# Two reorderings behind a two-layer expert stage: a transpose of gates moved behind one layer 1, a fold and a layer 2 moved ahead of the last layer 1

## The reference, cut to what matters

```python
x = x + attention(channel_layernorm(x))
t = tokens(x);  xt = layernorm(t)                  # the input of router and experts
probs = softmax(xt @ Wr + br); top_p, top_idx = top_k(probs, 2); weights = top_p / top_p.sum()
xn = layernorm(xt);  xe = xn * ln_g[e] + ln_b[e]   # for each expert e
h = gelu(xe @ W1[e] + b1[e]);  y[e] = h @ W2[e] + b2[e]
t = t + (weights[..., None] * y_tok[top_idx]).sum()
```

## Time and profile before

| what | us |
|---|---|
| median of 3 runs | 58.93 (58.92 to 59.0) |
| the profiled execution | 59.4 |
| its span from first to last instruction | 57.6 |
| PE busy | 50.3 (87%) |
| DVE busy | 40.9 (71%) |
| ACT busy | 35.4 (62%) |
| POOL busy | 24.8 (43%) |

### The profile page before, as it was taken

The page is one execution under the profiler, slowest core; times in us unless marked ns, Lnnn a source line. Parts: engine busy times, 40 slices in busy tenths (PEclk is TensorE's granted clock), DMA queues, the critical chain, the costliest instruction groups (busy, mean ns, idle before and its releaser), DMA issues.

```text
span 57.6 us, 1641 instructions
## 1 busy us (share of the span) xinstructions
PE 50.3 (87%) x556; PEld 29.9 (52%) x556; DVE 40.9 (71%) x175; ACT 35.4 (62%) x79; POOL 24.8 (43%) x49
## 2 busy tenths in 40 slices
PE   1997999999869999999999769999999779999520
PEld 0332656985756986762484344544746344335510
DVE  3198478697999798897389999088390769949630
ACT  5500377991693959979889667688797898000000
POOL 6239761000059989939199900004968000053000
PEclk9999999999999999999999999999999999999999
DMA  0442448981000000000000461368894000110012
GB/s 0 108 106 26 103 120 239 332 330 60 0 6 11 0 0 0 0 11 6 0 11 6 165 182 40 142 196 242 275 270 148 13 0 6 58 33 0 0 36 55
DMA packets 4584, 4.80 MB, mean 83 GB/s; under 512 B 2204, under 2 KB 3040, under 8 KB 4576
## 3 DMA queue, kind: packets, MB, share of 16 engines
q1 hardware_dynamic: 4256, 4.67, 26.9%
q10 hardware_dynamic: 320, 0.03, 0.5%
HBM read 4.41 MB, written 0.29 MB: 82 GB/s over the span
## 4 chain that ended last, share of the span: by engine, by line
PE 65%; DVE 19%; issue 6%; DMA 3%; POOL 1%; ACT 1%; DVEq 0%; ACTq 0%; POOLq 0%
PE banks L1056 18%; PE banks L1084 13%; PE banks L1097 6%; PE banks L990 4%; PE banks L1037 4%; PE banks L963 4%; DMA X<-in_x_dram 3%; PE banks L1126 3%; PE banks L926 2%; PE banks L942 2%; DVE PTS L612 2%; PE banks L1140 2%; PE banks L950 1%; DVE nmax L607 1%; PE banks L933 1%
## 5 line engine op out<-in xcount | busy, mean ns | idle before, releaser
L492 ACT ACTIVATE H<-banks,PF 128x512 f32<-128x512 f32 x32 | 19.7, 687 | 2.6 <-PE banks L1056 1.9
L1056 PE MATMUL banks<-XE,W1F 64*64 64x256 f32 x224 | 14.3, 381 | 0.7 <-ACT H L492 0.7
L1056 PEld LDWEIGHTS banks<-XE,W1F 64*64 64x64 f32 x224 | 8.8, 133 | 5.2 <-issue 3.5
L385 POOL TENSOR_TENSOR acc<-acc,gated 128x512 f32<-128x512 f32 x4 | 5.5, 1367 | 13.6 <-DVE gated L746 7.0
L1084 PE MATMUL banks<-H,W2F 64*64 64x512 f32 x80 | 9.6, 593 | 0.0
L368 POOL TENSOR_SCALAR XE<-XF,PF,LB 128x256 f32<-128x256 f32 x14 | 7.7, 562 | 1.4 <-ACT XF L470 1.4
L735 DVE TENSOR_TENSOR YS<-banks,YA 128x512 f32<-128x512 f32 x5 | 3.5, 690 | 5.2 <-ACT YA L502 5.2
L926 PE MATMUL banks<-zeros 128*128 128x512 f16 x13 | 5.5, 562 | 1.3 <-POOL zeros L387 1.3
L346 POOL TENSOR_TENSOR rs<-base,half 128x2 f32<-128x2 f32 x4 | 2.8, 700 | 8.7 <-DVE base L648 8.5
L1084 PEld LDWEIGHTS banks<-H,W2F 64*64 64x64 f32 x80 | 3.2, 133 | 3.7 <-issue 3.4
L453 ACT ACTIVATE PR<-banks,nmax 128x256 f32<-128x256 f32 x8 | 3.8, 480 | 1.7 <-DVE nmax L607 1.7
(11 more groups left out here) (93 smaller groups left out, 81.1 us busy)
## 6 DMA issues: line engine op xcount, KB each, us to landing
GS<-gates_kept SPq DMA_DIRECT2D x14, 128.0 KB, 3.1
W1F<-in_w_dram SPq DMA_DIRECT2D x1, 768.0 KB, 4.7
W2F<-in_w_dram SPq DMA_DIRECT2D x1, 512.0 KB, 4.8
G<-gates_kept SPq DMA_DIRECT2D x2, 256.0 KB, 4.3
W1F<-in_w_dram SPq DMA_DIRECT2D x1, 256.0 KB, 3.2
out_dram<-res SPq DMA_DIRECT2D x4, 64.0 KB, 1.6
X<-in_x_dram SPq DMA_DIRECT2D x2, 64.0 KB, 2.0
X<-in_x_dram SPq DMA_DIRECT2D x1, 128.0 KB, 2.4
```

The source lines that it names most:

```text
L385: nc.gpsimd.tensor_tensor(acc[h][:, :], acc[h][:, :], gated[s % 2][:, :], ALU.add).then_inc(acc_ready, 1)
L492: nc.scalar.activation(H[:, r, :].rearrange("p (t n) -> p t n", t=PT), ps_z[z_slot(g // J)][:, :, PIX * j:PIX * j + PIX], ACT.Gelu, bias=P ...
L1056: mm = nc.tensor.matmul(ps_z[z_slot(q)][C * c:C * c + C, k, PIX * j:PIX * j + PIX], W1F[rows, e, j, C * c:C * c + C], XE[h][rows, e, :], s ...
```

## The change

TensorE: `layer1(8)` is issued ahead of `turn_gates(1)`; `fold_sum` and `layer2(5)` are issued ahead of `layer1(15)`. ScalarE: `gelu(15)` stands ahead of its copy `turn_gates(1)`. VectorE: `finish_part` and `finish_first` stand ahead of `weigh_last(0)`, and `weigh(5)` ahead of `weigh_last(2)`. No instruction is added or removed.

```diff
@@ ScalarE's order
             gelu(14)
+            gelu(15)
             turn_gates(1)
-            for g in range(15, 18):
-                gelu(g)
+            gelu(16)
+            gelu(17)
             keep_part(2)
@@ VectorE's order
             weigh(4)
+            finish_part()
+            finish_first()
             weigh_last(0)
             weigh_last(1)
-            finish_part()
-            finish_first()
+            weigh(5)
             weigh_last(2)
             weigh_last(3)
-            weigh(5)
             weigh(6)
@@ TensorE's order
             layer1(7)
+            layer1(8)
             turn_gates(1)
-            layer1(8)
             layer2_split(2)
@@ TensorE's order, further down
             layer1(13)
             layer1(14)
-            layer1(15)
             fold_sum()
             layer2(5)
+            layer1(15)
             layer2(6)
```

## The result

The changed kernel takes 58.53 us (median of 20; 58.23 to 59.29), the kernel before 59.07 beside it: a ratio of 0.9889 (0.9858 to 0.992). The forecast was 0.44 us less than before; the medians differ by 0.54. The ratios and their intervals leave out executions more than 1.5% above the fastest of their kernel, so they are not the ratio of the two medians; one of those left out, of the second edit alone, took 266.84 us.

What follows compares the result with a forecast made beforehand. TensorE's in-order issue, with breaks of 0.97 and 0.66 us, and at the end VectorE's strand too, bound the kernel. 0.47 from the first break and -0.03 from the second give 0.44: 58.93 - 0.44 = 58.49 us, range 57.95 to 58.75.

Steps and rivals of the forecast that it cites:

- First edit: TensorE, layer1(8) ahead of the gates' transpose: layer2_split(2) starts 0.47 us sooner, held by sum_parts(1); bounds 0 and 0.91.
- The copy of the gates: ScalarE, now behind gelu(15): the copy starts 0.08 us later than 34.01.
- the spreads: Gate loads of pairs 2 to 7 on SyncE's queue: shift by 0.08 us, last six covered, nothing counted.
- The loop: Split layer 2, kept part, sum, next split: the turn stays 3.63 us and all moves with its start.
- Second edit, the hold: VectorE's weigh_last(2) waits for GpSimd's add_up(5), takes 1.1 us and ends 0.56 us behind it; chance 0.62.
- The sum: Whole kernel: 0.42 to 0.46 us sooner, taken as 0.44; median 58.49.
- the second edit's tail: Kernel's end after moving fold_sum and layer2(5) ahead of layer1(15), with weigh_last(2) blocked: -0.03 us.
- the rest is the same: Behind add_last(1): fold_last(1), the result and the store are as before.
- No hold: weigh_last(2) runs free beside add_up(5) or misses it: 0.89 us sooner, 58.04; chance 0.21, including a small part of the wait.
- First edit void: layer2_split(2) still starts at 34.81: 58.96, no change that can be told; chance 0.09.
- The clock: TensorE's clock falls from 2.4 to 1.2 GHz ahead of layer2_last: 60.6; chance 0.08, shared with unseen causes.

Runs made afterwards that it cites:

- the second edit alone: Kernel before with only fold_sum and layer2(5) ahead of layer1(15) and VectorE's order to match; run twice: ratio 1.0044, then 0.9963.
- the first edit alone: Kernel before with only layer1(8) ahead of the gates' transpose and gelu(15) ahead of the copy: ratio 0.9912, 23.33 us from layer1(7).

## Why the prediction was right, point by point

- **First edit: right.** 0.47 us of the 0.97, limited by `sum_parts(1)` behind the router chain. Alone it gave 0.47, and with that sum moved forward the limit moved with it. The copy of the gates did not even come 0.08 later: 33.55 - 33.23 = 0.32 behind the transpose, 0.33 before. The row that the forecast called on for the spreads shows no transfer from 45.00 to 46.00 only, not from 45.00 on the earlier trace rows; nothing came to hang on it.
- **The loop: right.** 37.52 - 33.88 = 3.64 a turn. `fold_sum` follows `layer1(7)` by 44.77 - 31.18 = 13.59 us; forecast 45.22 - 31.64 = 13.58. No weighing waited for a spread.
- **Second edit, the hold: right.** `weigh_last(2)`, forecast to take 1.1 us, took 0.98; it ends 0.55 behind `add_up(5)`; the row of before gave 0.56. The overlap was shorter than forecast (0.43 instead of 0.59), because `layer1(15)` followed `layer2(5)` by 1.87, not 1.77, and `gelu(30)` was late with it. That cost nothing, since GpSimd's end counts and not the start of the wait. The run without `add_up(5)` shows the price, 0.30 us. The two instructions share no semaphore, so "meet only at semaphores" in the first section is too strong. The idle time of TensorE ahead of `layer2_last`, forecast at about 1 us, reads 0.71 because the row counts from the modelled end of `layer2(6)`; counted as the forecast did it is 50.90 - (48.25 + 1.72) = 0.93. What the page SBUF — State Buffer of the Trainium skill says in its section Who interferes with whom, on two SBUF inputs against a reading GpSimd, held here too; its full block, taken to the letter, would have ended `weigh_last(2)` 0.13 us later (49.69 + 0.68 = 50.37 instead of 50.24).
- **The sum: 0.14 too small by the trace** (0.44 against 0.58). The term that was mis-sized is the second edit's tail, forecast at -0.03 and measured at 0.11 to 0.13. Its parts: the pair of `weigh_last` ended 50.85 - 44.77 = 6.08 behind `fold_sum`, not 6.11; `layer2_last` followed by 0.05, not 0.10; `add_last(1)` ended 53.35 - 50.90 = 2.45 behind that, not 2.42. The largest is the last: "the rest is the same" was wrong. From the end of `add_last(1)` to the start of the last result it took 55.15 - 54.27 = 0.88 us before and 54.11 - 53.35 = 0.76 after. Why that got shorter was not tested. Together, with 0.01 lost ahead of `fold_sum`, the parts lead from the 0.42 of the steps to 0.58.
- **The median: close by luck.** 58.53 lies 0.04 from the forecast 58.49, but only because the kernel before came out at 59.07 in 20 executions, 0.14 above the 58.93 that the forecast started from. The gain itself is 0.54 by medians, 0.58 by the trace.
- **Rivals.** No hold: refuted by the 0.98 us and by the run without the add. First edit void: refuted. The clock: the two halves of `layer2_last` take 1.95 us, before 1.90, so no halved clock behind the 0.71 us break; the granted clock reads 1.00 from 50.90 to 54.10.

## What to carry to other kernels

Time freed on an in-order engine is worth only what lies up to the next semaphore: list every wait of the instruction that would move up, and take the latest. A break is best filled with work that just fits it; what is longer (`layer2(5)` here) pushes back the producer behind it, and its consumers on other engines become the end. Before VectorE work with both inputs in SBUF is moved, look at what GpSimd will be doing at that moment.

## What the runs showed of the hardware that I had not expected

The same first instructions, ahead of all the edits, take a different time from one execution to the next. Between the first two transposes stand three matmuls on zeros (128x512, f16) whose result nobody uses; they keep TensorE at work ("warming"). Their rows on TensorE's timeline, in the first edit alone, in the changed kernel, and the single one of the run with one (a second row shows the last two of the three by themselves):

```profile
5.43 1.49 PE L927 MATMUL banks<-zeros 128*128 128x512 f16 x3
...
5.86 1.06 PE L927 MATMUL banks<-zeros 128*128 128x512 f16 x2
```

```profile
5.36 0.81 PE L927 MATMUL banks<-zeros 128*128 128x512 f16 x3
...
5.57 0.59 PE L927 MATMUL banks<-zeros 128*128 128x512 f16 x2
```

```profile
5.55 0.54 PE L927 MATMUL banks<-zeros 128*128 128x512 f16 x1
```

In the nine traces with three of them whose first transpose began between 5.18 and 5.27 us, `layer1(7)` started at 31.13 to 31.39 where they took 0.81 to 0.95 us, at 31.64 to 31.69 where they took 1.14 to 1.16, at 31.80 with 1.33 and at 31.98 with 1.49: the later part moves with them. The starts of the first two lie 0.43 us apart in the slow trace (5.43 and 5.86) and 0.21 in the quick one (5.36 and 5.57), a factor of two as between TensorE's 1.2 and 2.4 GHz. The profile's clock reads 1.00 throughout these stretches, so the clock itself is not shown. The Trainium skill (TensorE: Matmul & The Clock Gate, section Wait — 56ns, not 53.3ns?) gives 426.7 and 215.7 ns from start to start for 512 columns at the two levels, which agrees. Of the 1.1 us between the two profiled spans, 0.46 lie ahead of both edits and are not the change's; that they come from the moment at which the clock rose is argued from the factor of two, not shown.
